# Moving the two value products of an attention head in between its exponentials, the second one a head later

## The reference

```python
w = (xn @ W.T).reshape(B, T, 16, 128).transpose(0, 2, 1, 3)
q, k, v = rms_norm(w, g1), rms_norm(w, g2), rms_norm(w, g3)
att = einsum('bhid,bhjd->bhij', q, k) / sqrt(128)
score = softmax(att, axis=-1) + softmax(att, axis=-2)
y = einsum('bhij,bhjd->bihd', score, v).reshape(B, T, C)
s = y @ W
g = silu(ffn(xn))        # silu(xn @ w_gate) * (xn @ w_up), @ w_down, with scales
return x + s * g
```

## Time and profile before

| | us |
|---|---|
| two timed runs | 3333.13, 3357.58 |
| their median | 3345.36 |
| the profiled execution | 3337.44 |
| its span (slowest core, core 5) | 3335.8 |
| spans of the 8 cores | 3316.9 to 3335.8 |
| attention stage, about | 437 to 1424 of the span |

### The profile page before, as it was taken

The page is one execution under the profiler, slowest core; times in us unless marked ns, Lnnn a source line. Parts: engine busy times, 40 slices in busy tenths (PEclk is TensorE's granted clock), DMA queues, the critical chain, the costliest instruction groups (busy, mean ns, idle before and its releaser), DMA issues.

```text
span 3335.8 us, 29507 instructions; the slowest of 8 cores (3316.9 to 3335.8 us)
## 1 busy us (share of the span) xinstructions
PE 2498.7 (75%) x11176; PEld 1024.1 (31%) x11176; DVE 565.1 (17%) x1171; ACT 823.5 (25%) x1306; POOL 138.2 (4%) x222
## 2 busy tenths in 40 slices
PE   2787766676666666659999998666769999967564
PEld 0333322222222222224444443222224444422221
DVE  0222221221221221201122221010022222200101
ACT  2555545546546456400011000000000000000000
POOL 0000000000000000000000000111100000011010
PEclk9888866676676676779999999988989999999898
DMA  8111000000000000060533333545553333255553
GB/s 165 39 51 38 13 0 1 1 1 0 1 1 1 1 0 1 1 114 38 202 151 152 152 152 126 177 176 199 179 191 155 154 155 153 102 201 188 191 187 140
DMA packets 56302, 329.17 MB, mean 99 GB/s; under 512 B 4961, under 2 KB 4961, under 8 KB 43873
## 3 DMA queue, kind: packets, MB, share of 16 engines
q0 software_dynamic: 48384, 285.23, 24.7%
q1 hardware_dynamic: 7778, 42.05, 3.5%
HBM read 197.24 MB, written 12.58 MB: 63 GB/s over the span
## 4 chain that ended last, share of the span: by engine, by line
PE 48%; DMA 24%; ACT 16%; issue 7%; DVE 5%; ACTq 0%; DVEq 0%; POOLq 0%; POOL 0%; PEldq 0%; SPq 0%
DMA wdb<-wd_in 20%; PE PS L614 13%; PE PS L620 13%; ACT Ei L386 9%; PE PS L265 8%; PE PS L438 4%; PE PS L491 3%; ACT escr L393 3%; PE PS L541 3%; DMA whT<-wt_in 2%; DVE vv L428 1%; PE PS L378 1%; ACT rnT L348 1%; PE PS L679 1%; DMA ws_lo<-ws_in 1%
## 5 line engine op out<-in xcount | busy, mean ns | idle before, releaser
L679 PE MATMUL PS<-wdb,fuse 128*128 128x512 bf16 x2048 | 533.7, 421 | 273.9 <-DMA wdb<-wd_in 249.4
L614 PE MATMUL PS<-xnT_lo,wgb 128*128 128x512 bf16 x2048 | 467.8, 382 | 23.0 <-DVE outs_t L710 19.1
L378 PE MATMUL PS<-rnT,rnTq 128*128 128x512 bf16 x768 | 336.8, 579 | 187.1 <-ACT escr L393 90.4
L620 PE MATMUL PS<-xnT_lo,wub 128*128 128x512 bf16 x2048 | 462.9, 379 | 0.0
L679 PEld LDWEIGHTS PS<-wdb,fuse 128*128 128x128 bf16 x2048 | 208.9, 106 | 598.7 <-issue 427.9
L386 ACT ACTIVATE Ei<-PS,nMu 128x1024 bf16<-128x1024 f32 x256 | 285.7, 1116 | 86.1 <-PE PS L378 64.9
L633 ACT ACTIVATE guscr<-PS,sgv 128x512 f32<-128x512 f32 x128 | 88.2, 689 | 796.9 <-PE PS L620 796.9
L614 PEld LDWEIGHTS PS<-xnT_lo,wgb 128*128 128x128 bf16 x2048 | 201.4, 98 | 269.9 <-issue 31.6
L620 PEld LDWEIGHTS PS<-xnT_lo,wub 128*128 128x128 bf16 x2048 | 200.4, 98 | 241.6
L702 ACT ACTIVATE outs_t<-scrA 128x2048 f32<-128x2048 f32 x8 | 15.3, 1911 | 819.0 <-DVE scrA L692 819.0
L638 DVE TENSOR_SCALAR guscr<-PS,suv 128x512 f32<-128x512 f32 x128 | 96.1, 751 | 698.0 <-ACT guscr L633 698.0
(11 more groups left out here) (89 smaller groups left out, 1336.9 us busy)
## 6 DMA issues: line engine op xcount, KB each, us to landing
wdb<-wd_in POOLq DMA_DIRECT2D x128, 1024.0 KB, 5.3
wgb<-wg_in POOLq DMA_DIRECT2D x32, 2048.0 KB, 7.4
wub<-wu_in POOLq DMA_DIRECT2D x32, 2048.0 KB, 11.9
x_t<-x_in SPq DMA_DIRECT2D x16, 1024.0 KB, 5.0
whT<-wt_in POOLq DMA_DIRECT2D x8, 1024.0 KB, 15.9
xr_t<-x_in SPq DMA_DIRECT2D x8, 1024.0 KB, 6.7
out<-outs_t SPq DMA_DIRECT2D x8, 1024.0 KB, 4.1
ws_lo<-ws_in POOLq DMA_DIRECT2D x4, 1024.0 KB, 12.5
```

The lines of the kernel that those rows point to most:

```text
L378: last = t.matmul(PS[:, pofs + 512 * n: pofs + 512 * (n + 1)], rnTq[:, 128 * rb:128 * (rb + 1)], rnT[:, 512 * n:512 * (n + 1)], start=True ...
L614: last = t.matmul(PS[:, pg:pg + 512], wgb[wbi][:, k, 128 * ib:128 * (ib + 1)], xnT_lo[:, k, 512 * sp:512 * (sp + 1)], start=(k == 0), stop ...
L620: last = t.matmul(PS[:, pu:pu + 512], wub[wbi][:, k, 128 * ib:128 * (ib + 1)], xnT_lo[:, k, 512 * sp:512 * (sp + 1)], start=(k == 0), stop ...
L679: last = t.matmul(PS[:, pofs + 512 * n:pofs + 512 * (n + 1)], fuse[:, ic, 256 * tp + 128 * tb2:256 * tp + 128 * (tb2 + 1)], wdb[wbi][:, u, ...
```

## The change

- The loop over rb now also issues, for each rb, two matmuls of Y1 (of this head, after exponential rb) and two of Y2 of the head before (ahead of exponential rb). `pend` carries the head before; after the last head its Y2 is issued by a loop of its own. Y1 accumulates in PSUM 0 to 1023, Y2 in 2048 to 3071.
- Exponential rb waits for Y2's matmuls of block rb (`cur_y2c[rb]`), as it overwrites the block that they read.
- The scores have two areas of 1024 columns left, at 1024 and 3072. Blocks 0 to 7 alternate between them. For blocks 8 to 15 the own columns go to 1024 and the others to 3072, as two operations, each released by the exponential that read the area before.
- The three small exponentials go to the start of the head, `vv2`'s multiplies behind `rnTq`.
- The column sums go to PSUM 2560 and wait for the last exponential and the sum of the head before.
- `vv1`'s sixteen multiplies become sixteen operations, each with a semaphore and a wait.
- The sum `scY2` and its scaling are issued after block 15 of the next head.

The order on TensorE within one rb is: Y2 rb; scores rb+2 (for rb from 8 on the lower scores of rb+1); Y1 rb; from 8 on the upper scores of rb+1.

```diff
+        A("V", lambda v, h=h: [v.tensor_scalar_mul(
+            vv2[:, rb, :], rn[:, rb, 128 * h:128 * (h + 1)],
+            eMf[:, rb:rb + 1]) for rb in range(16)][-1], 1,
+          [("S", semf), ("T", prev_y1c15)])
+        vvv2 = M("V")
...
-                pofs = (rb % 2) * 1024
-                width = 1024
-                war = [("S", exp_done[rb - 2])] if rb >= 2 else []
-                if rb == 0:
-                    war += [("V", prev_scY1)]
-                elif rb == 1:
-                    war += [("V", prev_scY2)]
+                pofs = 1024 if rb % 2 == 0 else 3072
+                nr = (0, 1)
+            elif lo:
+                pofs, nr = 1024, (0, 1)
             else:
...
-            A("T", afn, 1, [("V", vq)] + war)
...
+            A("T", afn, 1, ws)
+            return M("T")
...
+        amark_lo[0] = a_block(0, True, [("V", vq)])
+        amark_lo[1] = a_block(1, True, [("V", vq), ("V", prev_fbcV)])
...
+        for rb in range(16):
+            if pend is not None:
+                def yfn(t, hp=pend["h"], rb=rb):
+                    last = None
+                    for n in range(2):
+                        last = t.matmul(
+                            PS[:, 2048 + 512 * n:2048 + 512 * (n + 1)],
+                            vv1[:, rb, :], Ei[:, rb, 512 * n:512 * (n + 1)],
+                            start=(rb == 0), stop=(rb == 15))
+                    return last
+                ws = [("V", pend["vv1m"][rb])]
+                if rb == 0:
+                    ws += [("V", pend["fbcV"]), ("S", trv[0])]
+                A("T", yfn, 1, ws)
+                cur_y2c[rb] = M("T")
+            slot = 1024 if (rb >= 8 or rb % 2 == 0) else 3072
+            ew = [("T", amark_lo[rb])]
+            if pend is not None:
+                ew.append(("T", cur_y2c[rb]))
+            A("S", lambda s, rb=rb, slot=slot: s.activation(
+                Ei[:, rb, :], PS[:, slot:slot + 1024], AF.Exp,
                 bias=nMu[:, rb:rb + 1], scale=1.0,
-                accum_out=S1[:, rb:rb + 1]), 1,
-              [("T", ta)] + ([("T", prev_y2T), ("V", prev_s1war)] if rb == 0
-                             else []))
+                accum_out=S1[:, rb:rb + 1]), 1, ew)
+            exp_mark[rb] = M("S")
             if rb >= 8:
-                A("S", lambda s, rb=rb, pofs=pofs: s.activation(
-                    escr[:, :], PS[:, pofs + 1024:pofs + 2048], AF.Exp,
+                A("S", lambda s, rb=rb: s.activation(
+                    escr[:, :], PS[:, 3072:4096], AF.Exp,
                     bias=nMu[:, rb:rb + 1], scale=1.0,
-                    accum_out=S2[:, rb:rb + 1]), 1)
+                    accum_out=S2[:, rb:rb + 1]), 1, [("T", amark_hi[rb])])
...
-        sexp_all = M("S")
-        A("S", lambda s: s.activation(eMb[:, :], nMu[:, :], AF.Exp, bias=0.0,
-                                      scale=consts[:, C_NEG1:C_NEG1 + 1]), 1)
-        semb = M("S")
...
+            if rb + 2 <= 7:
+                amark_lo[rb + 2] = a_block(rb + 2, True,
+                                           [("S", exp_done[rb])])
+            elif rb == 6:
+                amark_lo[8] = a_block(8, True, [("S", exp_done[6])])
+            elif rb == 7:
+                amark_hi[8] = a_block(8, False, [("S", exp_done[7])])
+            elif rb >= 8 and rb <= 14:
+                amark_lo[rb + 1] = a_block(rb + 1, True,
+                                           [("S", exp_mark[rb])])
+            def y1fn(t, rb=rb):
+                last = None
+                for n in range(2):
+                    last = t.matmul(PS[:, 512 * n:512 * (n + 1)],
+                                    vv2[:, rb, :],
+                                    Ei[:, rb, 512 * n:512 * (n + 1)],
+                                    start=(rb == 0), stop=(rb == 15))
+                return last
+            y1w = [("S", exp_mark[rb]), ("V", vvv2)]
+            if rb == 0:
+                y1w.append(("V", prev_scY1))
+            A("T", y1fn, 1, y1w)
+            y1c_mark[rb] = M("T")
+            if rb >= 8 and rb <= 14:
+                amark_hi[rb + 1] = a_block(rb + 1, False,
+                                           [("S", exp_done[rb])])
+            if pend is not None and rb == 15:
+                A("V", lambda v: v.tensor_tensor(
+                    scY2[:, :], scY1[:, :], PS[:, 2048:3072], ALU.add), 1,
+                  [("T", cur_y2c[15])])
+                A("V", lambda v, hp=pend["h"]: v.tensor_scalar_mul(
+                    y_st[:, hp, :], scY2[:, :], gv[:, 3:4]), 1)
+                prev_scY2 = M("V")
...
-        A("T", csfn, 1, [("S", semb)])
+        A("T", csfn, 1, [("S", semb), ("S", exp_done[15]), ("V", prev_scY2)])
...
-        A("V", vv2fn, 1, [("S", semf)])
-        vvv2 = M("V")
...
-        A("T", y1fn, 1, [("V", vvv2), ("S", sexp_all)])
-        ty1 = M("T")
...
-        def vv1fn(v, h=h):
-            last = None
-            for rb in range(16):
-                last = v.tensor_scalar_mul(vv1[:, rb, :],
-                                           rn[:, rb, 128 * h:128 * (h + 1)],
-                                           rS[:, rb:rb + 1])
-            return last
-        A("V", vv1fn, 1)
-        vvv1 = M("V")
...
+        vv1m = []
+        for rb in range(16):
+            vw = [("T", cur_y2c[rb])] if pend is not None else []
+            A("V", lambda v, rb=rb, h=h: v.tensor_scalar_mul(
+                vv1[:, rb, :], rn[:, rb, 128 * h:128 * (h + 1)],
+                rS[:, rb:rb + 1]), 1, vw)
+            vv1m.append(M("V"))
...
-                                         ALU.mult), 1, [("T", ty1)])
-        prev_scY1 = M("V")
...
-            return last
-        A("T", y2fn, 1, [("V", vvv1)])
-        prev_y2T = M("T")
-        A("V", lambda v: v.tensor_tensor(scY2[:, :], scY1[:, :], PS[:, 1024:2048],
-                                         ALU.add), 1, [("T", prev_y2T)])
-        prev_scY2 = M("V")
...
+                                         ALU.mult), 1, [("T", y1c_mark[15])])
+        scY1m = M("V")
...
+        prev_y1c15 = y1c_mark[15]
+        pend = {"h": h, "vv1m": vv1m, "fbcV": fbcV}
...
+    fl = {}
+    for rb in range(16):
...
+        ws = [("V", pend["vv1m"][rb])]
+        if rb == 0:
+            ws += [("V", pend["fbcV"]), ("V", prev_scY2)]
+        A("T", yfn, 1, ws)
+        fl[rb] = M("T")
+    A("V", lambda v: v.tensor_tensor(scY2[:, :], scY1[:, :], PS[:, 2048:3072],
+                                     ALU.add), 1, [("T", fl[15])])
+    A("V", lambda v: v.tensor_scalar_mul(y_st[:, 15, :], scY2[:, :],
+                                         gv[:, 3:4]), 1)
```

More of the change, by code:

```diff
@@ L327, in build @@
     prev_scY2 = 0
+    prev_tcs = 0
+    prev_tft = 0
+    prev_y1c15 = 0
+    pend = None
     trv = [0, 0]
     for h in range(NH):
+        A("S", lambda s: s.activation(eMb[:, :], nMu[:, :], AF.Exp, bias=0.0,
+                                      scale=consts[:, C_NEG1:C_NEG1 + 1]), 1,
+          [("V", prev_s1war), ("T", prev_tcs)])
+        semb = M("S")
+        A("S", lambda s: s.activation(eMf[:, :], nMu[:, :], AF.Exp, bias=0.0,
+                                      scale=consts[:, C_NEG1:C_NEG1 + 1]), 1)
+        semf = M("S")
+        A("S", lambda s: s.activation(eNg[:, :], nMu[:, :], AF.Exp, bias=0.0,
+                                      scale=1.0), 1)
+        seng = M("S")
         for grp in range(4):
@@ L449, in build @@
         A("V", lambda v: v.tensor_add(Sc[:, 8:16], S1[:, 8:16], S2[:, 8:16]), 1)
+        A("V", lambda v: v.reciprocal(rS[:, :], Sc[:, :]), 1)
+        A("V", lambda v: v.tensor_mul(fcol[:, :], eNg[:, 0:8], rS[:, 0:8]), 1,
+          [("T", prev_tft)])
         s1war = M("V")
-        A("V", lambda v: v.reciprocal(rS[:, :], Sc[:, :]), 1)
-        A("V", lambda v: v.tensor_mul(fcol[:, :], eNg[:, 0:8], rS[:, 0:8]), 1)
         A("V", lambda v: v.tensor_copy(fbf[:, :], fcol[:, :]), 1)
         vf = M("V")
-        def vv1fn(v, h=h):
-            last = None
-            for rb in range(16):
-                last = v.tensor_scalar_mul(vv1[:, rb, :],
-                                           rn[:, rb, 128 * h:128 * (h + 1)],
-                                           rS[:, rb:rb + 1])
-            return last
-        A("V", vv1fn, 1)
-        vvv1 = M("V")
+        vv1m = []
[5 more added lines that the diff above has]
+            vv1m.append(M("V"))
         def ftfn(t, h=h):
@@ L472, in build @@
         tft = M("T")
[L473 removed]
+        A("V", lambda v: v.tensor_copy(frow[:, :], PS[0:1, 2560:3584]), 1,
+          [("T", tft)])
         vfrow = M("V")
@@ L481, in build @@
         tfbc = M("T")
[L482 to L483 removed]
+        A("V", lambda v: v.tensor_copy(f_bc[:, :], PS[:, 2560:3584]), 1,
+          [("T", tfbc)])
+        fbcV = M("V")
         A("V", lambda v: v.tensor_tensor(scY1[:, :], PS[:, 0:1024], f_bc[:, :],
[L485 to L504 removed]
+                                         ALU.mult), 1, [("T", y1c_mark[15])])
+        scY1m = M("V")
```

(17 more changed lines are left out.)

76 lines of the change are left out of this document (17 added, 59 removed).

## The result

| | before | changed |
|---|---|---|
| median of all timed runs, us | 3348.5 | 3551.1 |
| the profiled execution, us | 3337.4 | 3556.4 |
| attention stage, first to last exponential, core 0, us | 951.6 | 1156.2 |
| a head's period, us | 61.5 | 75.1 |
| the rest of the program, core 0, us | 2371 | 2364 |

The change makes the kernel slower: the ratio to before is 1.0592, with an interval of 1.0561 to 1.0624, some 198 us, or 3535 us against 3337. (Some executions of every kernel run a few per cent longer with a lower clock on one die; the ratios leave them out, the medians of the table do not.) All of it is in the attention stage, from the first exponential to the last, which grew by 200 to 205 us on each of the eight cores.

The account below looks back on a forecast made before the run. ScalarE's exponentials bound the loop before; changed, the engines alternate. Loop 66.29 + tail 19.46 = period 85.75 us, 24.28 more, counted 15 times: +364, -1 at the end, 3337.4 + 363 = 3700 us; range 3470 to 3800, forecast's own 3640 to 3750.

Parts of the forecast that it names:

- step at low clock, first half: Loop steps 0 to 7: wait 1.36, six matmuls 2.72 at 1.2 GHz, 0.15 to ScalarE; 4.23 us in place of 1.30.
- step at high clock, first half: Loop steps 0 to 7: wait 1.36, six matmuls 1.45 at 2.4 GHz, 0.15 to ScalarE; 2.96 us in place of 1.30.
- step at high clock, second half: Steps from 8 to 15: TensorE waits for the second exponential, 2.66, then four matmuls 1.02 and 0.15; 3.83 us, before 2.60.
- vv1's sixteen multiplies: Tail, VectorE: between 2.69 us as before and 16 x 0.36 = 5.76 when each waits for the one ahead; upper end taken.
- last exponential to first, mean: The tail between two heads' loops, which both products leave: 19.46 us against 28.25 before.
- low steps of the first eight: Steps 0 to 7 of each head's loop: all 8 taken at low clock, 8 x 4.23 = 33.84 us.
- low steps of the last seven: Steps from 8 to 15 of each head's loop: 2.5 taken at low clock (5.08 us each), 4.5 at high (3.83).
- ScalarE and TensorE take turns: Loop: Y2 that exponential rb+1 waits for is queued behind matmuls waiting for exponential rb; loop 66.29 us against 33.22.
- low step of the second half: Steps from 8 to 15 at low clock: all eight matmuls run end to end, 1.36 + 3.57 + 0.15 = 5.08 us.
- Which clock?: Loop: bursts of six leave steps 0 to 7 low; from block 8 bursts of eight raise it, 2.5 steps low, 4.5 high.
- The rival of high clock throughout: Whole loop at 2.4 GHz: loop 53.00, tail 18.19, period 71.19 us, +145, 3482 us; chance 0.25 (throughout or nearly).
- the high case: Loop without long idle gaps between bursts keeps the clock high, by the skill's page; 3482 us would then be the forecast.

Follow-up runs that it names:

- e1_order: The changed kernel with Y2's matmuls of block rb+2, not rb+1, issued in step rb; ratio 0.9554 to the kernel before, period 52.6 us.
- e3_y2block: The changed kernel with all 32 Y2 matmuls of the head before issued at once ahead of the loop, Y1 left in it; period 56.0 us, profiled execution 3281.8 us.
- e5_five: The changed kernel with one Y1 matmul left out in each of blocks 0 to 7, so bursts of five (result not the reference's); ratio 1.0945 to before.
- e4_fill: The changed kernel with 21 matmuls per head that nothing reads, added in the tail to keep TensorE busy; ratio 1.0423 to before, period 71.6 us.
- e9_seven: The changed kernel with one score matmul of blocks 0 to 7 issued twice: bursts of seven, leading burst eight, steps 6 and 7 six; ratio 1.0621 to before.

## Why the prediction was right, and where it was not

The direction, the place and the mechanism held: slower, within the range, by steps in which the engines wait for each other. The likeliest time was 3700 us, and the measured 3551. By the terms of the sum, per head:

| term | predicted | measured |
|---|---|---|
| step at low clock, first half | 4.23 | 4.22 |
| step at high clock, first half | 2.96 | 2.96 |
| step at high clock, second half | 3.83 | 3.82 |
| vv1's sixteen multiplies | 5.76 | 5.69 |
| last exponential to first, mean | 19.46 | 19.77 |
| low steps of the first eight | 8 | 1.7 |
| low steps of the last seven | 2.5 | under 0.1 |
| steps 0 to 8, sum | 33.84 | 25.82 |
| steps 8 to 15, sum | 29.94 | 26.91 |

- **The queue order.** "ScalarE and TensorE take turns": 441.7 us of ScalarE's idle time ended with Y2's matmuls, and e1_order and e3_y2block take it away by the order alone.
- **The prices** of the steps came from rows of before and are right to 0.01 us, also the 5.08 of a low step of the second half, which e5_five shows. What an operation costs at a known clock carried over to an order that had never run.
- **The step that failed** is the answer to "Which clock?": "Bursts of six with gaps of 1.7 us are no longer than anything that left the clock low in the earlier trace rows; I take steps 0 to 7 as low." The longest burst that I had seen leave it low was of four, the shortest that I had seen raise it was of eight. Six lay between, and I took it for low without a row for it. With six it rose after none to three bursts in the heads of the profiled core; with five, in e5_five, it never did. So 6.3 steps of the first half were priced 1.27 us too long and 2.4 of the second 1.25: 8.0 + 3.0 = 11.0 us per head, 165 us, as much as 3700 - 3535. The tail, 0.3 us longer than forecast, is 5 us the other way, and the first head's loop about 2 us shorter.
- **The rival of high clock throughout** gave 3482 us and a chance of 0.25, and is nearer (69 us off) than the forecast (149). What it lacked is the first one or two steps and the first burst at low clock: 1.7 x 1.27 + 1.27 = 3.4 us per head, 51 us; e4_fill took 3.5 us per head off. A forecast for one clock or the other in each half was the wrong form: the two cases are joined by when the rise comes.
- **vv1.** I took the upper end, from the dependent pair, 5.76; it was 5.69. By the Trainium skill's page (VectorE: DVE Perf Modes, The DRAIN you can't avoid) the semaphores would have cost nothing. That does not hold for these operations: 2.69 us as one and 5.69 as sixteen, in both kernels. The difference may be that here each also waits for the one ahead; no run separates semaphore and wait. The 0.168 us between the grouped multiplies is 2.69 / 16; their starts in the trace are 0.163 apart.
- **The clock's rule.** By the Trainium skill's TensorE: Matmul & The Clock Gate, Why this matters for your kernels, long idle gaps between bursts make the clock fall, and I took from it the high case. The trace agrees in part: once high, the clock stayed to the end of the loop, through gaps of 1.50 us, in 14 of 15 heads. But it also fell with no longer gap ahead of it, in the head shown above and in e5_five (from 499.3 on), and e5_five, with the same gaps, stayed low for all its eight steps. The rule is of the fall, too, and most heads here begin low, so by itself it could not give the high case: short gaps alone did not bring the clock back.
- **vv2, the small exponentials and the sum of Y2** were costed at nothing, and no wait on them appears ahead of the exponentials: 441.7 of 445.6 us are Y2's.
- **The first head** and the end: the loop of head 0 is 28.6 us from exponential 0 to 15 on core 0, 2 less than before, and the last Y2 alone took 9.10. With the last two exponentials the first is 31.1, where I had said near 33. The end, from the last exponential to the last result, was 25.4 us against 25.66, where I had said 1 less.

## What to carry to other kernels

When work is moved in between the steps of a pipeline, write down the order in the queue and follow one full round of waits: if what step n+1 waits for is queued behind something that waits for step n, the two engines take turns, and one more step of lead removes it (here from +5.9% to -4.5%). An edit that costs nothing beside a long operation can cost its full length once that operation is moved away. And a burst length for which no row shows the clock is an open question, to be carried as a range or measured, not assumed.

## What the runs showed of the hardware

- In bursts that repeat every 3 to 5 us, one matmul of 512 columns made a difference to the clock: with five per burst it never rose from 1.2 to 2.4 GHz in the eight steps (120 low steps of 120 on the profiled core) and, where a head began high, it fell in the second step; with six it rose after none to four bursts (25 and 26 low). Less work made the kernel slower: 1.0945 against 1.0592.
- A leading burst of eight matmuls instead of six: the clock was high by the first burst of the loop in 108 of 120 heads instead of 17 (e9_seven against the changed kernel, all cores).
- Matmuls that nothing reads, 21 per head, put into TensorE's idle time, made the kernel faster by 3.5 us per head (e4_fill).
- Sixteen multiplies of 128 x 128 on VectorE: 0.163 us apart in one operation, 0.364 apart with a semaphore and a wait for each.
- From the end of an exponential (the read of its sum) to the matmul it releases 0.14 us, and from the end of a matmul, as the profile models it, to the exponential 0.14 to 0.16, at both clocks.
